# Moving the loads of the node rows from SyncE's DMA queue to ScalarE's in a graph-network kernel

## The reference

```
x = x + gnn0(layernorm(x))       # relu(A_norm (x W) + b), self loops, degree scaling on both sides
x = x + sliced_attention(layernorm(x))
x = x + hypergraph(layernorm(x)) # two graph products with weights W1 and W2
x = x + experts(layernorm(x))    # 8 experts, top 2, gelu
```

## Time and profile before

| what | value |
|---|---|
| median of 3 runs | 1354.86 us (1354.66 to 1356.01) |
| the profiled execution | 1354.04 us |
| its span, first to last instruction | 1352.3 us |
| PE busy | 1219.9 us, 90% of the span |
| DVE busy | 570.7 us, 42% |
| ACT busy | 473.6 us, 35% |
| POOL busy | 198.8 us, 15% |
| mean granted TensorE clock | 0.946 of full |

### The profile page before, as it was taken

One profiled execution on the slowest core, in us unless ns is written; L12 is line 12 of the kernel. 1 busy time (PEld: TensorE's weight loads), 2 busy tenths in 40 slices (PEclk: granted clock), 3 DMA queues, 4 the chain that ended last, 5 costly groups with the idle time before them and its releaser, 6 DMA issues. The chain is left out here.

```text
span 1352.3 us, 19576 instructions
## 1 busy us (share of the span) xinstructions
PE 1219.9 (90%) x7295; PEld 838.1 (62%) x7295; DVE 570.7 (42%) x1529; ACT 473.6 (35%) x1142; POOL 198.8 (15%) x201
## 2 busy tenths in 40 slices
PE   2399999979989999999999999999999519999993
PEld 1277777735547644457777544467777418888882
DVE  5878777557754513123333332223222552222221
ACT  5665666267733687830000010001222202222220
POOL 3000000023310000000000000000000014777772
PEclk8599999989999999999999999999999758999997
DMA  5132133400003155575565454587653074666665
GB/s 177 36 122 74 61 112 123 157 7 0 1 0 124 28 169 149 156 157 122 126 137 127 129 163 146 146 185 170 149 113 101 1 230 122 155 148 152 149 155 125
DMA packets 253782, 159.11 MB, mean 118 GB/s; under 512 B 171665, under 2 KB 242497, under 8 KB 253486
## 3 DMA queue, kind: packets, MB, share of 16 engines
q1 hardware_dynamic: 242606, 141.84, 37.7%
q0 software_dynamic: 11072, 15.90, 6.6%
HBM read 81.68 MB, written 38.28 MB: 89 GB/s over the span
## 5 line engine op out<-in xcount | busy, mean ns | idle before, releaser
L970 PE MATMUL bank<-weights,agg_in_out 128*128 128x320 f16 x2000 | 274.8, 299 | 0.0
L984 PE MATMUL bank<-weights 128*128 128x512 f16 x1250 | 271.0, 379 | 1.0 <-issue 0.8
L970 PEld LDWEIGHTS bank<-weights,agg_in_out 128*128 128x128 f16 x2000 | 195.7, 98 | 76.2
L984 PEld LDWEIGHTS bank<-weights 128*128 128x128 f16 x1250 | 121.8, 98 | 149.5 <-DVEq L1776 2.1
L1107 PE MATMUL bank<-weights,agg_in_out 128*128 128x320 f16 x1000 | 164.4, 301 | 0.0
L800 POOL TENSOR_TENSOR shift<-shift,rstd 128x5 f32<-128x5 f32 x15 | 3.7, 245 | 921.9 <-ACT rstd L805 921.9
L515 ACT CAST weights<-bank 128x500 f16<-128x500 f32 x160 | 114.3, 722 | 70.4 <-PE bank L504 70.4
L1107 PEld LDWEIGHTS bank<-weights,agg_in_out 128*128 128x128 f16 x1000 | 92.2, 98 | 26.7
L2248 PE MATMUL bank<-weights 128*128 x448 | 105.4, 384 | 0.4 <-ACT weights L2264 0.2
L2233 PE MATMUL bank<-wk,weights 128*128 128x256 f32 (+1 forms) x512 | 104.8, 359 | 0.9 <-DVE wk L2279 0.9
L2264 ACT ACTIVATE weights<-bank,weights 128x256 f32<-128x256 f32 (+1 forms) x128 | 50.2, 443 | 155.6 <-PE bank L2233 155.5
(11 more groups left out here) (353 smaller groups left out, 1422.0 us busy)
## 6 DMA issues: line engine op xcount, KB each, us to landing
weights<-counts_source_target SPq DMA_DIRECT2D x50, 800.0 KB, 4.6
counts_source_target<-weights SPq DMA_DIRECT2D x5, 4000.0 KB, 13.9
weights<-in_L_ffn_W SPq DMA_DIRECT2D x32, 512.0 KB, 3.8
weights<-in_L_ffn_W SPq DMA_DIRECT2D x4, 1024.0 KB, 5.6
rows_and_gates<-normed SPq DMA_DIRECT2D x1, 3300.0 KB, 12.0
token_out<-residual SPq DMA_DIRECT2D x1, 3200.0 KB, 20.1
out<-token_out SPq DMA_DIRECT2D x1, 3120.0 KB
residual<-in_x SPq DMA_DIRECT2D x4, 640.0 KB, 7.9
```

The source lines that it names most:

```text
L970: last = nc.tensor.matmul(bank, source[:, 5 * k + c, part * F + fh * P:part * F + fh * P + P], MB[:, k, c, h * HALF:(h + 1) * HALF], start ...
L984: last = nc.tensor.matmul(ps[j][:, :], MB[:, k, c, j * P:(j + 1) * P], source[:, 5 * k + c, :], start=(k == 0 and c == 0), stop=(k == 4 an ...
```

## The change

ACT issues all six loads of x, ahead of its first cast. SP no longer issues any of them: it issues the padding keys, waits for `y_ready`, and stores the keys. Nothing else is changed, and the semaphores are the same.

```
         def front_act(act):
+            for g in range(5):
+                n = 5 if g < 4 else 4
+                act.dma_start(XR[:, 5 * g:5 * g + n, :],
+                              x[5 * g * P:(5 * g + n) * P, :].rearrange("(c p) f -> p c f", p=P)
+                              ).then_inc(x_gr[g].sem, 16)
+            act.dma_start(XR[0:LAST, NC - 1, :], x[(NC - 1) * P:N, :]).then_inc(x_gr[4].sem, 16)
             nc.scalar.copy(triple[:, :, 2], ed[:, 1]).then_inc(y_ready.sem, 1)
...
         def front_sp(sp):
-            def rows(g):
-                n = 5 if g < 4 else 4
-                sp.dma_start(XR[:, 5 * g:5 * g + n, :],
-                             x[5 * g * P:(5 * g + n) * P, :].rearrange("(c p) f -> p c f", p=P)
-                             ).then_inc(x_gr[g].sem, 16)
-
             sp.dma_start(packed_dram[E * KW:(E + P) * KW].rearrange("(p j) -> p j", p=1), padkeys[0:1, :]
                          ).then_inc(st.sem, 16)
-            rows(0)
-            rows(1)
             sp.wait_ge(y_ready.sem, 3)
             sp.dma_start(packed_dram[0:E * KW].rearrange("(p j) -> p j", j=EW * KW),
                          triple[0:ER].rearrange("p j w -> p (j w)")).then_inc(st.sem, 16)
-            for g in range(2, 5):
-                rows(g)
-            sp.dma_start(XR[0:LAST, NC - 1, :], x[(NC - 1) * P:N, :]).then_inc(x_gr[4].sem, 16)
```

## The result

The changed kernel takes 1358.01 us, the median of 7 runs (1356.64 to 1360.44); the kernel before, run beside it, 1354.66 (7 runs, 1352.46 to 1357.31). The ratio is 1.0027, with a 95% interval of 1.0016 to 1.0039: some 3.7 us slower, 2.2 to 5.3. The forecast of 1355.6 had the direction and not the size. The time lies inside the stated range only because rivals B and C had widened it; the forecast's own range was - 1 to + 2.5. By its own signs the forecast as a whole was wrong: the time moved by more than 2.7 us, and the store took over 9.5.

A forecast was written before the change was run, and what follows sets the result against it. PE bounds the kernel from 69 us; before that, a start-up path of key words, store, first gathers and DVE's chain. + 2.8 - 2.1 = + 0.7 on 1354.86 gives 1355.6 us; own range - 1 to + 2.5, over all 1352.6 to 1359.0.

The forecast's parts named there:

- B: ACT's issuing: ACT is held while x moves, last issue let go at 18.5; + 3.7, 1358.6 us; chance 0.12.
- C: Keys' store: queues not separate in effect, it waits for all of x and takes 11.3 us; + 3.5, 1358.4; chance 0.13.
- its own signs: Whole forecast: wrong if time moves by more than 2.7 us, or moves with DVE's chain in its old place.
- Step 1: ACT's six issues ahead of its casts: 6.3 us, so ACT is free at 14.2.
- rival A: ACT's queue takes the six loads quickly, store goes at 12.3; - 3.5 to - 0.5, say 1352.9 us; chance 0.2.
- Step 2: ACT's casts: third key word ready at 15.7 instead of 11.83, so the store is issued 3.8 us later.
- Step 4: POOL's gathers: x is in before they start, all land in about 3.0 to 3.1 us; 2.1 us come back.
- step 3: Keys' store from issue to POOL's start: 8.5 us instead of 9.5; gathers start at 24.2, 2.8 us later than before.
- A store alone would take 7.2 us: Keys' store with nothing beside it: 4.9 us of data plus 2.3 us of fixed cost, worked out from the edge lists.
- Step 5: The sum on DVE's chain, hence on the whole: + 2.8 - 2.1 = + 0.7 us.
- under DVE's and ACT's work until 69 us: Cover for SP's weight loads, starting at 32.7 instead of 30.0 with the last gather's landing; said to cost nothing.
- the 1356.6: Time by the skill's rule that all DMAs share 16 engines: no gain in the store's time, + 3.8 - 2.1 = + 1.7 us.

The follow-up runs named there:

- casts first: The changed kernel with ACT's two casts ahead of its six loads of x; ratio to the kernel before 1.0008.
- casts late: The kernel before with six casts of zeros on ACT ahead of its first cast, no DMA moved; ratio 1.0003.
- before with the store cut: The kernel before with the keys' store cut in two, 112 partitions and 13; ratio 0.9985.
- before, store alone: The kernel before with SP waiting for the keys' store to land before it issues groups 2 to 4; ratio 1.0010.
- changed, two loads, casts, four: The changed kernel with ACT issuing groups 0 and 1, then its casts, then the other four loads; ratio to the kernel before 1.0000.
- before, all of x ahead on SP: The kernel before with all six loads of x issued by SP ahead of the wait for the key words; ratio 1.0031.
- the changed kernel with the cut store: The changed kernel with the keys' store cut into 112 partitions and 13; ratio to the kernel before 0.9997.

## Why the forecast missed: the store's bytes on its five DMA engines, and its late first packet

**What was right.** That the front sets the whole: PE's long run starts 3.66 us later and the time is 3.7 us longer. *Step 1*: 6.3 us of issuing were forecast, from 8.02 to ACT's first cast at 14.07 it is 6.0. The six issues took 0.44, 0.54, 0.55, 1.05, 1.54 and 1.74 us: the queue slows the issuer down as it did on SP, and ACT's casts paid for it. That took rival A's ground away, and B's too: ACT was never held to 17.7. *Step 2*: the store was forecast for 15.7 and left at 15.39. *Step 4*: 2.1 us were to come back behind the gathers, 2.0 did, with the first landing at 3.3 us where 3.0 was said. The runs in which x still moved past the gathers, with the store uncut or cut (casts first, casts late, before with the store cut), confirm it from the other side: landings of 5.7 to 5.9 us, and nothing back.

**The step that failed is step 3**, the store's time, taken at 8.5 us where 10.9 was measured. It holds two errors.

The first is 1 us of price. "A store alone would take 7.2 us" was worked out from the edge lists to SP's release, and is right for that (7.3); POOL starts 0.9 us behind it. The store alone is 8.2.

The second, of 1.4 us, is the wait and the sharing. By queue, or by packet size where both are on one queue (4.8 KB for keys, 1 KB for x), the store's time falls into three parts (us):

| kernel | issue to first packet | first to last packet | last packet to POOL |
|---|---|---|---|
| before, store alone | 2.0 | 4.9 | 1.4 |
| before | 1.7 | 6.5 | 1.3 |
| changed | 3.5 | 6.1 | 1.3 |
| changed, two loads, casts, four | 4.2 | 6.4 | 1.4 |
| changed, casts first | 4.4 | 5.7 | 1.4 |
| before, all of x ahead on SP | 5.2 | 6.9 | 1.4 |

From before to changed, the first column grows by 1.8 us and the second shrinks by 0.4: the store waits longer for its first packet. Here the forecast had 2.0 us (data from 17.7), and 3.5 was measured; it had about 1.3 us of sharing on top of the 4.9 of data, and 1.2 was measured, but with x's last rows on one engine and not with x on all 16. The 1.5 us of the first column are this second error, against which the data's 0.1 less hardly counts.

The forecast knew that the store runs on about five DMA engines, but asked when x would be gone from all 16 together ("to 18.9"; the stretches have it at 19), and let the store share "for a little over a microsecond". What counts for the end is the load of each of those five. Of x they carry a sixteenth each, 3.15 MB / 16 = 197 KB; of the store a fifth, 600 KB / 5 = 120 KB. At the 24 GB/s of the lone engine in the tail these 317 KB last 13.2 us, and counted from about 10.3, where the loads of x near their full rate (some 250 GB/s from 10 to 11), that ends at 23.5; the stretches have the five engines stop at some 23.6. One engine has x's last 53 rows besides, 54 KB, and its 371 KB end at 25.8; the tail stops at almost 26.0. While x moves on all 16 engines, these five are as busy as the rest, so the store's own 4.9 us of data come on top wherever it stands in the order. Queues change only whose bytes are last. In one queue, with all of x ahead, it is the store's, and POOL starts at 27.46; on two queues the store's data take turns with x's last rows on one engine, and POOL starts at 26.30 (24.79 with the last rows issued behind the store). Cut over 16 engines, the store puts 37 KB on each: 234 KB, 9.8 us, an end at 20.1; the changed kernel with the cut store has all engines busy to 20, the store's last packet at 21.3 and POOL at 22.71. The same sum fits these three kernels, and the one cut is worth the loss of the change (1.0027 to 0.9997). The one-queue run that loses as much shows that x ahead of a store on five engines is enough for the loss; the cut in both kernels puts its share at about half, and 1.7 us are left that go with the later issue and that no run takes apart. That the first packet takes 3.4 to 4.4 us from the issue in every kernel with x on ACT's queue, even while x is still far from through, and not over 2.0 with at most two row groups ahead of it on the one queue, is measured; its mechanism stays open.

The Trainium skill has the rule behind the numbers five and one: "DMA: Bandwidth & Descriptors", section "Why a DMA increments its semaphore by 16 and not by 1", says that a DMA runs on the largest number of engines, up to 16, that divides the outer sizes of both its sides. It gives five for 125 partitions and one for 53 rows; the trace agrees (shares of 0.33 and 0.06), and so do the cut kernels.

**Step 5** then read + 0.7 on DVE's chain, and + 2.9 is what the profile has at keys 1. To that comes a term that the forecast did not have: 0.7 us more ahead of L663. It had named SP's weight loads as "under DVE's and ACT's work until 69 us", free of cost. They start later in the changed kernel, with the last gather, and so come to lie in that gap (DMA share 0.67 instead of 0.12). That cover failed; the instruction packet in the gap is a candidate and no more. 2.9 + 0.7 is the 3.66 at PE.

**The rivals.** C came nearest: all of x passes first, + 3.5, 1358.4; measured 1358.01. Its mechanism was the right one in the main ("the share of a third speaks against it" was the argument misread: the share of a third is what makes it so), though its 11.3 us were borrowed from another load, and x's last rows on one engine did not pass first. The store's first packet at 18.9, with x all but through, is what C said; in the kernels that issue the store earlier it starts while x still moves, so it is no rule. B's + 3.7 has the size by another road. The rule of the Trainium skill that the prediction cites ("DMA: Bandwidth & Descriptors", section "Issuing engines are not separate DMA queues") had the right side, and the 1356.6 worked out by it was still 1.4 us short: on two queues side by side the store took 11.4 and 12.0 us from an issue at 12, 1.9 and 2.5 more than on one. The chance given to C and B together, 0.25, was too small beside 0.76 for no change that can be told.

**From the front to the end.** PE's start is not the whole story inside the profile. Its granted clock stands at half, 1.2 GHz, when the long run begins, and rises to 2.4 GHz between 72 and 73 us in the kernel before, 3.0 us after the start, and between 78 and 79 in the changed one, 5.4 us after. The first stretches of either, before first:

```profile
71.00:72.00 1.00, 1.00 (x8) 0.66 (x6) 0.93 (x3) 0.62 (x1) 0.00 (x0) 0.50 0.00 0
72.00:73.00 1.00, 1.00 (x11) 0.78 (x10) 0.29 (x2) 0.25 (x2) 0.00 (x0) 0.95 0.00 0
```
```profile
77.00:78.00 1.00, 1.00 (x6) 0.56 (x4) 0.76 (x2) 0.72 (x1) 0.00 (x0) 0.50 0.00 0
78.00:79.00 1.00, 1.00 (x11) 0.73 (x10) 0.30 (x1) 0.30 (x1) 0.00 (x0) 0.94 0.00 0
```

By the last of these products (near 265 and 270 us) the changed kernel is 4.8 us behind, and at the next stage's start (411.7 and 414.4) 2.7 again: from 390 to 400 it has the full clock and the kernel before 0.83. The spans differ by 2.6 us, 1354.9 and 1352.3. In fourteen profiles of nearly the same kernel this rise came 2.4 to 5.6 us after the start of the run, in no order that follows the edits. A single profile is therefore uncertain by a microsecond or two at the end, and I rest nothing on differences between runs that are smaller than that, the 0.7 us gap at L663 in the total among them.

## What to carry to other kernels

Multiply the DMA share of a stretch in which nothing else moves by 16: it says on how many engines a transfer runs, and a transfer that gates the critical path should run on all of them; 112 and 13 partitions instead of 125 were worth 2 us here on the store alone, 3 with the edge lists. Add up the bytes engine by engine, with everything that shares them, before moving a load to another queue: the queue changes the order, not the sum, and here the second queue also made the first packet late. Look at the packets by queue before explaining a slow transfer: the time from issue to POOL alone had pointed to sharing by bytes, where the packets took turns. And count what a queue that pushes back does to the engine that issues: six loads kept ACT from two casts for six microseconds.

## What the runs showed of the hardware beyond that

- POOL started its indirect DMA 0.9 to 1.0 us after the event that released it, whether that was a DMA's semaphore (19.19 to 20.08, by SP's release) or DVE's (17.05 to 18.04, 17.52 to 18.52). Behind the store's last packet it starts 1.3 to 1.4 us later.
- With packets of both queues waiting, an engine took one of each in turn (23 of the store's and 24 of x's from 19 to 20 us in the run with two loads, the casts, then four). The store's first packet started 3.4 to 4.4 us behind its issue in the six kernels with x on ACT's queue, and 1.2 to 2.0 in those with at most two row groups ahead of it on SP's.
- ACT issued five loads of x in 4.24 us in the changed kernel and in 8.63 us with the casts first, where the store was issued among them; three loads issued just ahead of the store, with two long under way, took 1.53 us.
- A gap of DVE ahead of L663, in which it waits for no semaphore, grows from about 2 us (1.86 to 2.43) to 2.6 to 3.7 with loads in flight.
- The clock's rise, above: 2.4 to 5.6 us into the same run of products.
